# Attention with relative positions on one core: two sets of probability buffers, the maximum rows moved ahead of the second turned scores

## What is computed

```python
# x: (2, 2048, 256); 16 heads of 16; relative_k, relative_v: (511, 16)
xn = layernorm(x)
Q, K, V = heads(xn @ Wq.T + bq), heads(xn @ Wk.T + bk), heads(xn @ Wv.T + bv)
rel_pos = arange(L)[None, :] - arange(L)[:, None] + 255      # negative rows wrap, the rest is clamped
scores = einsum('bhld,bhrd->bhlr', Q, K) / 4
scores = scores + einsum('bhld,lrd->bhlr', Q, relative_k[rel_pos])
attn = softmax(scores)
out = einsum('bhlr,bhrd->bhld', attn, V) + einsum('bhlr,lrd->bhld', attn, relative_v[rel_pos])
x = x + merge(out) @ Wo.T + bo + experts(xn)                 # 8 experts, top 2
```

## Time and profile before

| what | us |
|---|---|
| runs, median of 3 | 3551.71 (3551.53 to 3552.87) |
| the profiled execution, its own time | 3552.47 |
| its span, first to last instruction | 3550.7 |
| busy in the span: PE, DVE, ACT, POOL | 3083.0, 2884.8, 2729.6, 2415.4 |
| first and last L1188 (one per unit, 512) | 181.8, 2955.8 |
| mean granted TensorE clock | 0.938 of 2.4 GHz |

### The profile page before, as it was taken

The page is one execution under the profiler, slowest core; times in us unless marked ns, Lnnn a source line. Parts: engine busy times, 40 slices in busy tenths (PEclk is TensorE's granted clock), DMA queues, the critical chain, the costliest instruction groups (busy, mean ns, idle before and its releaser), DMA issues. The chain is left out here.

```text
span 3550.7 us, 148100 instructions
## 1 busy us (share of the span) xinstructions
PE 3083.0 (87%) x55702; PEld 2327.1 (66%) x55702; DVE 2884.8 (81%) x7981; ACT 2729.6 (77%) x6108; POOL 2415.4 (68%) x2654
## 2 busy tenths in 40 slices
PE   7588989898889898888898888889989896999990
PEld 4356666666666666666666666666666664579980
DVE  6488989999999999999989999989989996534443
ACT  3288888888888898888888888888888894334440
POOL 0177887888887888888888888888887875800006
PEclk9779999999999999999999999999999997589995
DMA  7766666666666666666666666666666664822214
GB/s 211 225 227 210 216 214 210 215 216 211 218 214 212 212 219 214 214 214 215 213 213 215 213 212 215 218 211 211 215 217 211 214 218 143 262 63 67 67 58 145
DMA packets 355891, 700.11 MB, mean 197 GB/s; under 512 B 59257, under 2 KB 168546, under 8 KB 354930
## 3 DMA queue, kind: packets, MB, share of 16 engines
q1 hardware_dynamic: 349042, 673.89, 58.9%
q0 software_dynamic: 6144, 16.79, 1.4%
HBM read 342.99 MB, written 347.46 MB: 194 GB/s over the span
## 5 line engine op out<-in xcount | busy, mean ns | idle before, releaser
L857 POOL TENSOR_TENSOR pt_near<-pt_full,pt_near 128x512 f16<-128x512 f32 (+3 forms) x1984 | 1849.0, 962 | 521.3 <-DVE pt_near L1198 521.3
L1095 ACT ACTIVATE pt_full<-pb,exp_bias 128x512 f32<-128x512 f32 x2048 | 1346.0, 695 | 299.4 <-POOL pt_near L857 118.3
L1178 DVE TENSOR_REDUCE part_max<-pb 128x1 f32<-128x512 f32 (+3 forms) x1376 | 768.6, 572 | 102.3 <-PE pb L939 100.1
L1174 DVE CUSTOM_DVE_ANT_0 near_sum<-pb,skewed 128x512 bf16<-128x512 f32 (+3 forms) x1216 | 674.6, 570 | 87.3 <-PE pb L939 65.4
L973 PE MATMUL pb<-ident,skewed 128*128 128x128 f32 x3840 | 646.5, 290 | 69.8 <-ACT q_max L1119 45.1
L1029 PE MATMUL pb<-pt_near,table_pair 128*128 128x64 f16 (+6 forms) x18432 | 646.5, 188 | 3.1 <-DVE rel_out L1230 3.1
L1029 PEld LDWEIGHTS pb<-pt_near,table_pair 128*128 128x128 f16 x18432 | 576.0, 97 | 76.2 <-issue 72.5
L1005 PE MATMUL pb<-v_head,pt_near 128*128 128x33 f16 x13440 | 544.7, 178 | 92.2 <-POOL pt_near L857 73.9
L1005 PEld LDWEIGHTS pb<-v_head,pt_near 128*128 128x128 f16 x13440 | 446.6, 96 | 191.0 <-POOL pt_near L857 109.9
L1198 DVE CAST pt_near<-pt_full 128x512 f16<-128x512 f32 (+3 forms) x1280 | 538.2, 470 | 0.0
L973 PEld LDWEIGHTS pb<-ident,skewed 128*128 128x128 f32 x3840 | 421.3, 144 | 111.6 <-ACT q_max L1119 69.6
(11 more groups left out here) (182 smaller groups left out, 4187.8 us busy)
## 6 DMA issues: line engine op xcount, KB each, us to landing
skewed<-rel_scratch SPq DMA_DIRECT2D x256, 576.0 KB, 5.4
rel_scratch<-rel SPq DMA_DIRECT2D x416, 319.5 KB, 3.2
rel_scratch<-rel SPq DMA_DIRECT2D x320, 320.0 KB, 2.7
skewed<-rel_scratch SPq DMA_DIRECT2D x64, 512.0 KB, 4.5
skewed<-rel_scratch SPq DMA_DIRECT2D x64, 448.0 KB, 4.2
k_stack<-planes_scratch SPq DMA_DIRECT2D x192, 96.0 KB, 4.8
planes_scratch<-planes SPq DMA_DIRECT2D x64, 256.0 KB, 2.3
rel_scratch<-rel SPq DMA_DIRECT2D x64, 256.0 KB, 2.9
```

The costliest lines, as they stand in the source:

```text
L857: ins = nc.gpsimd.tensor_tensor(pt_piece(c, 1, a, z, near), pt_full[e][:, (a - 4 * g) * P:(z - 4 * g) * P], pt_piece(c, 0, a, z, near), AL ...
L1095: nc.scalar.activation(pt_full[e][:, :], x_ps[e % 2][:, :], ACT.Exp, bias=exp_bias[:, 0:1]).then_inc(s_exp, 1)
L1174: ins = nc.vector.tensor_tensor_reduce(out=near_sum[:, col:col + z - a], in0=src, in1=skewed[k % 4][:, col:col + z - a], scale=1.0, scalar ...
L1178: ins = nc.vector.tensor_reduce(best, src, axis=AX.X, op=ALU.max)
```

## The change

It does four things.

1. `pt_full` becomes two sets of four buffers, taken in turn by units. The exponential of unit u waits for the low part of unit u - 2 instead of u - 1.
2. A cast whose blocks are all near no longer waits for the value products of the unit before. By `pieces` these are 6 of 16 units for e = 0, 6 for e = 1, 6 for e = 2 and 3 for e = 3.
3. TensorE issues `max_rows` behind the first two value products and ahead of the second pair of turned scores, instead of behind that pair and its score banks. The place of the maximum in the rotation of banks moves with it.
4. ScalarE copies `q_max` ahead of the exponentials 2 and 3, instead of behind them.

```diff
 def bank_items(k):
-    return [("scores", k - LAG_S, 0), ("scores", k - LAG_S, 2), ("rel", k, 0), ("rel", k, 1),
-            ("scores", k - LAG_S, 1), ("scores", k - LAG_S, 3), ("max", k - LAG_A, 0)] + \
+    return [("scores", k - LAG_S, 0), ("scores", k - LAG_S, 2), ("rel", k, 0), ("rel", k, 1), ("max", k - LAG_A, 0),
+            ("scores", k - LAG_S, 1), ("scores", k - LAG_S, 3)] + \
         [("pick", k - LAG_SEL, n) for n in range(PICK_BANKS) if (k - LAG_SEL) % HALF_C == 0]
...
-        pt_full = [sb(f"pt_full{i}", [P, CH]) for i in range(E)]
+        pt_full = [[sb(f"pt_full{b}{i}", [P, CH]) for i in range(E)] for b in range(2)]
...
         def wait_pt_free(eng, it, u, e):
-            if u >= 1:
+            if u >= 1 and not all(near for _, _, near in pieces(u % NB, GROUP_ORDER[e])):
                 eng.wait_ge(s_pv, it * (4 * STEP) + 4 * (u - 1) + e + 1)
...
-                    if pair and exists(it, k - LAG_A):
-                        max_rows(it, k - LAG_A)
                     if summing:
                         values(it, k - LAG_PV, 2 * pair)
                         values(it, k - LAG_PV, 2 * pair + 1)
+                    if pair == 0 and exists(it, k - LAG_A):
+                        max_rows(it, k - LAG_A)
...
             def exponentials(it, u, e):
-                if u >= 1:
-                    wait_low(act, it, u - 1, e)
-                nc.scalar.activation(pt_full[e][:, :], x_ps[e % 2][:, :], ACT.Exp, bias=exp_bias[:, 0:1]).then_inc(s_exp, 1)
+                if u >= 2:
+                    wait_low(act, it, u - 2, e)
+                nc.scalar.activation(pt_full[u % 2][e][:, :], x_ps[e % 2][:, :], ACT.Exp, bias=exp_bias[:, 0:1]).then_inc(s_exp, 1)
...
+                if exists(it, k - LAG_A):
+                    query_rows(it, k - LAG_A)
                 if turning:
                     exponentials(it, k - LAG_X, 2)
                     exponentials(it, k - LAG_X, 3)
-                if exists(it, k - LAG_A):
-                    query_rows(it, k - LAG_A)
                 if turning:
                     high_part(it, k - LAG_X, 2)
                     high_part(it, k - LAG_X, 3)
```

More of the change, by code:

```diff
@@ L857, in low_part @@
                     ins = nc.gpsimd.tensor_tensor(
-                        pt_piece(c, 1, a, z, near), pt_full[e][:, (a - 4 * g) * P:(z - 4 * g) * P],
+                        pt_piece(c, 1, a, z, near), pt_full[u % 2][e][:, (a - 4 * g) * P:(z - 4 * g) * P],
                         pt_piece(c, 0, a, z, near), ALU.subtract)
@@ L1102, in high_part @@
                 for a, z, near in pieces(c, g):
-                    ins = nc.scalar.copy(pt_piece(c, 0, a, z, near), pt_full[e][:, (a - 4 * g) * P:(z - 4 * g) * P])
+                    ins = nc.scalar.copy(pt_piece(c, 0, a, z, near), pt_full[u % 2][e][:, (a - 4 * g) * P:(z - 4 * g) * P])
                 ins.then_inc(s_ha, 1)
@@ L1197, in high_part @@
                 for a, z, near in pieces(c, g):
-                    ins = nc.vector.tensor_copy(pt_piece(c, 0, a, z, near), pt_full[e][:, (a - 4 * g) * P:(z - 4 * g) * P])
+                    ins = nc.vector.tensor_copy(pt_piece(c, 0, a, z, near), pt_full[u % 2][e][:, (a - 4 * g) * P:(z - 4 * g) * P])
                 ins.then_inc(s_hd, 1)
```

## The result

The changed kernel takes 3571.51 us, the median of 5 runs (3567.59 to 3571.80), against 3551.53 us (3549.03 to 3552.87, 5 runs). The ratio is 1.0055, with a 95% interval of 1.0040 to 1.0069: slower by 20 us. The forecast was 3575 us and slower. The profiled execution has a span of 3569.8 us.

A forecast was written before the change was run, and what follows sets the result against it. Attention steps were taken as bound by a ring of waits through TensorE and ScalarE: 5.40 us plus 0.07 for GpSimd's burst, 5.475 against 5.43, x 512 = +23 us, giving 3575 us; range 3528 to 3622.

The forecast's parts named there:

- MAX ahead of T1: TensorE's second turned scores wait for ScalarE's low half of the maximum: 0.51 us later in even steps, 0.96 in odd.
- The lag in front of MAX: From the end of ScalarE's low half of the maximum to TensorE's maximum rows: taken as 0.14 us, lower bound 0.05.
- T1 to the next T0: TensorE from the second pair of turned scores to the next step's first pair: odd step 3.09 us, forecast 2.67.
- The ring: Loop of waits through ScalarE's exponentials and TensorE's turned scores that sets a step: forecast 5.40 us on its own.
- The burst: GpSimd's work without a pause over three steps, with v parts, mask and output: 1.2 us a head left.
- the slack of V1: How late the second value product may be on TensorE: about 1.0 us, read from an odd step.
- rival C: GpSimd's burst stays: second value product takes over the first exponential's wait, 3 us a head; 3630 us, chance 0.12.
- A: Faster, held exponentials were the price, at the burst and behind: 3460 us, chance 0.12; mild form 3520 to 3545, 0.14.
- B: Whole kernel: no net effect, within 0.2% (7 us); chance 0.12.
- D: VectorE's freed casts collide with GpSimd's subtractions in the burst: 0.18 us a step, 3667 us; chance 0.04.
- the sign of being wrong: TensorE's maximum rows (L953) waiting under 100 us in the attention phase would show the forecast wrong.
- The step behind the burst: Step after GpSimd's unbroken work, 6.30 us from first exponential to next first exponential: forecast to fall below 5.9.

The follow-up runs named there:

- e1: Kernel before with the two sets of pt_full alone: 3515.26 us, 0.9891.
- e3: Kernel before with the near casts alone not held by the value products: 3549.80 us, 1.0001.
- e11: Kernel before with two sets of pt_full, near casts not held, and GpSimd's value parts in eight steps without mask or output: 3448.77 us, 0.9716.
- e2: Kernel before with the order alone: moved maximum rows, their bank's place and the q_max copy; one set of pt_full: 3617.38 us, 1.0189.
- e10: Changed kernel with GpSimd's eight value parts one a step, in steps without mask or output: 3497.45 us, 0.9850.
- e9: Kernel before with two sets of pt_full and GpSimd's eight value parts one a step, in steps without mask or output: 3449.88 us, 0.9719.
- e4: Changed kernel with ScalarE's low half of the maximum (L1109) issued between exponentials 0 and 1: 3532.73 us, 0.9952.
- e7: Changed kernel with ScalarE's low half of the maximum ahead of take_low, still behind exponentials 0 and 1: 3551.75 us, 1.0004.
- e8: Kernel before with two sets of pt_full and ScalarE's low half of the maximum between exponentials 0 and 1: 3554.19 us, 1.0016.

## Why the prediction was right, and where it was right by luck

**Direction and size.** 3575 us was said, 3571.5 us came. The steps of the working came out unevenly, though, and TensorE's clock, which has a part in the loss, has no term in the sum.

**Two sets.** Said: between 0 and 120 us, the next late thing is V1. Shown by e1: 35 us, with L1005's wait up from 65.7 to 107.2 us.

**Near casts.** Said: nothing. Shown by e3 and again, with less cover, by e11.

**MAX ahead of T1.** Said: T1 waits for ML and for ScalarE's lag; this is what makes the change slower. That the moves are what costs is shown by e2 (67 us alone) and by e10 against e9 (48 us without a burst); that T1's wait for ML is in it by e4 (39 us back at the same clock when ML comes early). In the two steps worked out, E0 to ML was 1.72 us in the odd step, said 1.73. In the changed kernel's quiet steps T1 starts 1.90 us behind E0 in the odd step and 1096.81 - 1095.17 = 1.64 in the even one, where 1.99 and 1.72 were said. The lag in front of MAX was 1101.79 - 1101.73 = 0.06 us, not 0.14: the lower bound was the true one. T1 to the next T0 took 1104.38 - 1101.91 = 2.47 us, not 2.67: the row of before held other short gaps than the one taken out, between S1 and V2 and between V2 and L1029. So 5.48 against 5.79 in the odd step and 4.84 against 5.03 in the even one. **The ring was oversized by 0.2 to 0.3 us in a quiet step.**

**What else bounds a step.** The prediction set VectorE aside by a mean, 4.92 us busy. In five of the sixteen steps of a head of the kernel before, its pauses come to under 0.1 us (means over 27 heads, from one L1190 to the next). Two such steps, from the end of one L1190 to the next, in the kernel before and then in the changed one (columns as in the earlier trace rows, VectorE the third busy time):

```profile
1058.26:1063.72 5.46, 4.59 (x96) 3.65 (x93) 5.43 (x15) 4.67 (x10) 5.03 (x5) 1.00 0.78 253
1063.72:1069.27 5.55, 5.22 (x111) 3.76 (x111) 5.51 (x16) 4.90 (x12) 3.46 (x4) 1.00 0.61 208
```

```profile
1060.39:1065.86 5.47, 5.32 (x111) 4.08 (x105) 5.34 (x16) 4.77 (x11) 5.04 (x5) 1.00 0.85 264
1065.86:1071.40 5.54, 4.60 (x86) 3.58 (x86) 5.50 (x15) 4.90 (x12) 3.44 (x4) 0.83 0.51 189
```

They have the same length to 0.01 us: in this head the new wait costs nothing where VectorE sets the step. The second of these steps takes 5.54 or 5.55 us in all 27 heads before and in 26 of 27 in the change; the first is the subject of the next paragraph. VectorE was argued from its mean and should have been read step by step. It also fits e7's small gain.

**The clock.** The first of those two steps, read at the same place of each head, takes 5.46 to 5.53 us in all 27 heads of the kernel before that were read (heads 3 to 29). In the changed kernel it takes 5.46 or 5.47 us in 16 of them and 5.91 to 6.31 us in 11, and these 11 are the ones in which TensorE's granted clock fell there. Two heads of the changed kernel, each with the step ahead and this one (the clock third from the end):

```profile
441.21:446.42 5.21, 4.14 (x89) 3.30 (x84) 4.58 (x16) 5.17 (x12) 3.67 (x5) 0.85 0.59 190
446.42:452.46 6.04, 6.04 (x109) 4.58 (x107) 4.47 (x15) 4.56 (x10) 4.57 (x5) 0.85 0.68 217
```

```profile
529.40:534.60 5.20, 4.14 (x101) 3.14 (x97) 4.58 (x15) 5.16 (x12) 3.66 (x5) 1.00 0.57 188
534.60:540.06 5.46, 5.31 (x111) 4.07 (x105) 5.34 (x15) 4.77 (x11) 5.03 (x5) 1.00 0.79 242
```

TensorE is busy 4.14 us in the step ahead in both, where it was 4.66 us before, with the clock at full:

```profile
443.53:448.74 5.21, 4.66 (x107) 3.47 (x107) 4.48 (x15) 5.17 (x12) 3.67 (x5) 1.00 0.61 196
```

This place alone makes some 0.6 x 11 / 27 x 32 = 8 us, an estimate. From the first L1190 to the last TensorE stood at half its clock, 1.2 GHz, for 141 us before and for 185 us in the change, 271 us in e2, 124 us in e1, 132 us in e10 and 46 us in e9, by the clock records of the traces: each version with the moves has more of it than its partner without. By the 2 us for 0.001 of mean clock that the runs of e7 and e8 show, the change's 0.932 against 0.938 would be 12 of its 20 us. That is an estimate too. A lower clock can be both the cause of a longer run and the consequence of its waits, and no run separates the two; what is shown is that the price of the moves is not T1's wait for ML alone.

**The burst.** Said: 1.2 us a head are left of it. e10 shows 74 / 32 = 2.3 us a head, if all that the spread gains was the burst's; part of it is the clock, which rose from 0.932 to 0.939. **By that this term was too small by 1.1 us a head, some 36 us.** What is left with the burst away is the step that the prediction put at 5.40 us (it holds VectorE's steps and the clock as well, which the prediction's does not), by line 1187 of e10 (1188 there has moved up by one):

```profile
L1187 DVE TENSOR_REDUCE neg_max<-part_max x512: 156/158/161, 181.7 to 2900.6; 128x1 f32<-128x5 f32 x96, 128x1 f32<-128x6 f32 x43, 128x1 f32<-128x4 f32 x32
```

(2900.6 - 181.7) / 511 = 5.32 us, where 5.40 was said: 0.08 us a step too large, 41 us. The two errors have opposite signs and cancelled, and the clock had no term; the right total is in part luck. In the burst the step that failed was the slack of V1, taken as 1.0 us from a quiet step. At the end of the burst V0 waits as well, and MAX, T1 and Q stand behind both: rival C was nearer to what happened, in place, than the forecast.

**Rivals.** A (faster, the holds were the price) needed T1's delay to be under 0.3 us a step on average. Over the 27 heads T1 starts 1.28 us behind E0 on average before and 1.92 us in the change, 0.64 us later (0.43 in even steps, 0.87 in odd ones), so A fell by its own test. What the step has to pay for this delay is less: the moves cost 56 to 67 us, 0.11 to 0.13 us a step. The change is slower all the same, because the holds were worth 35 us and not 120. B and D fell.

**What was to be seen.** L953's wait for L1109 was forecast as 250 to 350 us over the phase and is 115.5 us, nearer to the sign of being wrong (under 100) than to the forecast, although T1's delay came nearly as said: TensorE's waits for V0 and V1 stand ahead of MAX and take up part of the time to ML's end. The waits for GpSimd's low parts at L1095 and for q_max at L973 are gone, as said. The step behind the burst did not fall below 5.9 us: it takes 7.16 us in the head shown. Part of that is what E0 no longer waits ahead of it: the step now begins earlier and waits inside.

**The Trainium skill's rule** that a VectorE instruction in a two-port mode and a GpSimd instruction exclude each other (SBUF — State Buffer, section Who interferes with whom) was weighed for the freed casts. The trace agrees with it: in the kernel before, all 157 of these casts over 0.8 us began while a GpSimd instruction ran and ended 0.22 to 0.29 us after it. The freed casts did not make it worse: the median is 413 to 417 ns and the longest cast 1262 to 1380 ns over the versions, and those over 0.8 us are 116 in the changed kernel.

## What to carry to other kernels

In a pipeline of in-order engines, an instruction moved forward takes its own wait with it, and everything behind it inherits that wait: ask what the moved instruction waits for, where that stands in the other engine's order, and what the instruction it overtakes had needed instead. A hold that is lifted is worth only the distance to the next consumer of the same late result; here it was a third of the wait in the profile. When four engines are each 80 to 90% busy, look for the steps in which one of them has extra work: spreading GpSimd's eight small parts over steps without other extras was worth nearly twice what the second set of buffers was. And read the granted clock beside every time: new waits on TensorE can cost more than their own length.

## What the runs showed of the hardware

The lag from the end of a ScalarE instruction to a matmul that waits for it is not one number, but two. Before, L953 started 0.14 us behind the copy L1087 in all 108 such waits of over 0.1 us; in the change it started 0.05 us behind ML in 341 of 342. The pair of instructions does not decide it: L973 behind an exponential took 0.04 us in all 69 waits before and 0.14 us in 67 of 68 in the change. What does was not tried.

TensorE's granted clock fell to half, 1.2 GHz, at the end of the burst of the kernel before, right after two waits of 0.97 and 0.75 us for GpSimd. The second row gives the same place of the changed kernel, with waits of 0.96 and 0.75 us, where it stayed at full, 2.4 GHz (columns as in the earlier trace rows, the clock third from the end):

```profile
1088.30:1090.50 2.20, 2.20 (x24) 1.35 (x24) 1.30 (x3) 2.20 (x6) 2.06 (x3) 0.50 0.24 38
```

```profile
1090.60:1092.50 1.90, 1.45 (x24) 0.97 (x24) 1.90 (x2) 0.42 (x2) 1.90 (x2) 1.00 0.71 234
```

The four transposes of T1 there took 1.10 us at 1088.42 in the kernel before, against 0.61 us at 1091.37 in the changed one. So waits of the same length don't cost the same each time. The mean granted clock of the spans was 0.938 before, 0.921 in e2 and 0.950 in e9.
